# Register tables of a graph kernel's SAGE items laid out at a stride of eight words per turn

## The reference, cut to what matters

```
x: (6250, 128); src, dst: (100000,), sorted by dst; edge attributes: (100000, 16)
h = x                                            # three SAGE layers
for i in range(3):
    agg = segment_sum(h[src], dst); cnt = segment_sum(1, dst)
    h = (agg / clip(cnt, 1)) @ Wl[i] + bl[i] + h @ Wr[i]      # relu after the first two
x = layernorm(x + h)
z = concat(x[dst], x[src], edge_attr)            # one gated convolution
msg = sigmoid(z @ Wf.T + bf) * softplus(z @ Ws.T + bs)
agg = segment_sum(msg, dst)                      # batch norm, + x, layer norm, relu, + x
out = layernorm(x + that)
```

## Time and profile before

| what | value |
|---|---|
| median of 3 runs | 3572.85 us (3572.25 to 3573.68) |
| span of the profiled execution | 4974.4 us |
| time around that span | not recorded |
| first gather, first item of layer 0 | 63.9 us, 147.4 us |
| last gather of layer 2 | 3206.7 us |
| convolution's gathers | 3321.2 to 4818.0 us |

### The profile page before, as it was taken

How to read it: one execution, slowest core, us unless ns; L and a number is a source line. 1 busy time by engine, 2 the same in 40 slices (tenths; PEclk the granted TensorE clock), 3 DMA queues, 4 the chain that set the end, 5 groups by cost and what they waited for, 6 DMA issues and landing times. The chain is left out here.

```text
span 4974.4 us, 71543 instructions
## 1 busy us (share of the span) xinstructions
PE 3115.4 (63%) x16221; PEld 2251.0 (45%) x16222; DVE 2208.2 (44%) x5207; ACT 1206.7 (24%) x1906; POOL 2285.5 (46%) x2399
## 2 busy tenths in 40 slices
PE   4457677556366665463566664566777677777775
PEld 4334444445244443462344444544555455555553
DVE  5633333334411212354333333455666566556667
ACT  1112222101000000000000000035555555556665
POOL 2245445462355554533555555425455555444530
PEclk7678888767677777776787776687888788888887
DMA  3242323211333433113455542143333333222321
GB/s 95 77 132 90 100 87 101 73 41 46 89 103 105 108 106 90 40 38 115 147 157 149 149 139 74 36 126 89 86 87 85 87 85 87 80 81 82 89 61 41
DMA packets 345804, 454.70 MB, mean 91 GB/s; under 512 B 135431, under 2 KB 260386, under 8 KB 342099
## 3 DMA queue, kind: packets, MB, share of 16 engines
q0 software_dynamic: 88624, 207.58, 15.5%
q10 hardware_dynamic: 101984, 181.27, 11.4%
q1 hardware_dynamic: 155092, 64.77, 5.0%
HBM read 357.03 MB, written 101.90 MB: 92 GB/s over the span
## 5 line engine op out<-in xcount | busy, mean ns | idle before, releaser
L722 POOL DMA_INDIRECT shared<-y_dram,idx x1584 | 1514.9, 956 | 1604.7 <-DMA idx<-ea_sb 995.4
L909 PE MATMUL ps<-shared,work 128*128 x4368 | 786.2, 330 | 558.7 <-issue 463.2
L762 POOL DMA_INDIRECT shared<-q_dram,idx x784 | 753.6, 961 | 762.7 <-SPq L618 523.7
L909 PEld LDWEIGHTS ps<-shared,work 128*128 128x128 f32 x4368 | 709.3, 239 | 642.6 <-issue 631.4
L1961 DVE TENSOR_TENSOR acc<-acc,ps 128x129 f32 x546 | 156.0, 286 | 1577.4 <-remote 771.3
L1113 PE MATMUL ps<-pq,work 128*128 x1664 | 584.0, 453 | 146.6 <-issue 57.9
L928 PE MATMUL ps<-pq,work 128*128 128x385 bf16 x1456 | 335.8, 376 | 214.7 <-issue 119.3
L1113 PEld LDWEIGHTS ps<-pq,work 128*128 128x128 f32 x1664 | 299.8, 225 | 257.4 <-issue 201.2
L2250 DVE TENSOR_TENSOR work<-ps,shared 128x256 f32<-128x256 f32 x832 | 294.9, 417 | 248.6 <-PE ps L1116 94.8
L1264 ACT CAST work<-ps 128x300 bf16<-128x300 f32 (+1 forms) x520 | 175.1, 423 | 618.0 <-PE ps L900 322.8
L1123 PE MATMUL ps<-ident,work 128*128 128x128 f32 x832 | 152.9, 315 | 273.7 <-DVE work L2264 252.5
(11 more groups left out here) (356 smaller groups left out, 4062.7 us busy)
## 6 DMA issues: line engine op xcount, KB each, us to landing
work<-counts_dram ACTq DMA_DIRECT2D x156, 384.0 KB
counts_dram<-work ACTq DMA_DIRECT2D x26, 1568.0 KB
shared<-y_dram,idx POOLq DMA_INDIRECT x1584
ea_parts<-work ACTq DMA_DIRECT2D x128, 196.0 KB
ea_sb<-ea_parts SPq DMA_DIRECT2D x196, 128.0 KB
work<-counts_dram ACTq DMA_DIRECT2D x52, 416.0 KB
shared<-q_dram,idx POOLq DMA_INDIRECT x784
y_dram<-work SPq DMA_DIRECT2D x21, 448.0 KB, 3.1
```

The costliest lines, as they stand in the source:

```text
L722: pool.indirect_dma_start(msg[:, u, 0:F], None, y_dram, bass.IndirectOffsetOnAxis(ap=idx[:, u:u + 1], axis=0)).then_inc(s_quad[q], 16)
L762: pool.indirect_dma_start(q_ring[:, u * 2 * F:(u + 1) * 2 * F], None, q_dram, bass.IndirectOffsetOnAxis(ap=idx[:, u:u + 1], axis=0)).then_ ...
L909: last = te.matmul(ps[:, SUM_BANKS[i], 0:FA], lhsT=oh4[:, OH_SLOTS[i], u, :], rhs=shared[:, bass.ds(place + u * FA, FA)], start=u == 0, st ...
```

## The change

The tables in `q_regs` are no longer a copy of the twelve rows. Each table that is read by turns has eight words per turn, of which seven are used, and begins at a multiple of four words. Nine copies on SyncE's queue, each from a part of one row, fill it in the place of one. Every load of seven words becomes a load of four and a load of three, each from a multiple of four words; SyncE's load of twelve becomes three of four. VectorE's three or two first columns have places of their own. The semaphore `tab_back` counts eight copies more. The arithmetic on data, the order of the items and all other instructions are as before.

```diff
+WIDE = 8
...
+TURNS_ALL = TURNS + DTURNS
+CONV_TURNS = NQ // RC - 1
+NEEDED_AT = 0
+PLACES_AT = NEEDED_AT + TURNS * WIDE
+COLS_AT = PLACES_AT + TURNS_ALL * WIDE
+PAIR_COLS_AT = COLS_AT + TURNS * WIDE
+FIRST_COLS_AT = PAIR_COLS_AT + DTURNS * WIDE
+FIRST_PAIR_COLS_AT = FIRST_COLS_AT + 4
+SUMS_AT = FIRST_PAIR_COLS_AT + 4
+SUMMED_AT = SUMS_AT + TURNS_ALL * WIDE
+CONV_DONE_AT = SUMMED_AT + QG
+Q_WORDS = CONV_DONE_AT + CONV_TURNS * WIDE
+Q_TABLES = [(NEEDED_AT, 0, 0, TURNS, IT, WIDE), (PLACES_AT, 1, 0, TURNS_ALL, IT, WIDE), (COLS_AT, 2, OHS - 1, TURNS, IT, WIDE),
+            (PAIR_COLS_AT, 2, NI1 + LOOK, DTURNS, IT, WIDE), (FIRST_COLS_AT, 2, 0, 1, OHS - 1, OHS - 1), (FIRST_PAIR_COLS_AT, 2, NI1, 1, LOOK, LOOK),
+            (SUMS_AT, 3, 0, TURNS_ALL, IT, WIDE), (SUMMED_AT + RQ - AHEAD, 4, 0, 1, QG - RQ + AHEAD, QG), (CONV_DONE_AT, 5, 0, CONV_TURNS, RC, WIDE)]
+TAB_Q = 16 + 16 * len(Q_TABLES)
+TAB_ALL = TAB_Q + 32
...
-        q_regs = sb("q_regs", [1, 6 * NIC * P], i32)
+        q_regs = sb("q_regs", [1, Q_WORDS], i32)
...
-            sp.dma_start(q_regs[:, :], q_regs_dram.rearrange("r p -> (r p)").rearrange("(o k) -> o k", o=1))\
-                .then_inc(s["tab_back"], 16)
+            for at_, row_, first_, turns_, n_, wide_ in Q_TABLES:
+                from_dram = bass.AP(q_regs_dram.tensor, q_regs_dram.offset + row_ * NIC * P + first_, [[NIC * P, 1], [n_, turns_], [1, n_]])
+                sp.dma_start(q_regs[0:1, at_:at_ + turns_ * wide_].rearrange("o (t e) -> o t e", e=wide_)[:, :, 0:n_] if turns_ > 1
+                             else q_regs[0:1, at_:at_ + n_].rearrange("o (t e) -> o t e", e=n_), from_dram).then_inc(s["tab_back"], 16)
...
             def load_items(first, a, b):
-                sp.reg_load(l_regs[a:b], q_regs[0:1, bass.ds(first, b - a)])
+                for k in range(a - a % 4, b, 4):
+                    lo, hi = max(a, k), min(b, k + 4)
+                    sp.reg_load(l_regs[lo:hi], q_regs[0:1, bass.ds(first + lo, hi - lo)])
...
                 def load_turn(it):
-                    pe.reg_load(t_regs, q_regs[0:1, bass.ds(it * IT, IT)])
-                    pe.reg_load(g_regs, q_regs[0:1, bass.ds(it * IT + NIC * P, IT)])
+                    for k in range(0, IT, 4):
+                        pe.reg_load(t_regs[k:k + 4], q_regs[0:1, bass.ds(it * WIDE + (NEEDED_AT + k), min(4, IT - k))])
+                        pe.reg_load(g_regs[k:k + 4], q_regs[0:1, bass.ds(it * WIDE + (PLACES_AT + k), min(4, IT - k))])
...
             def load_columns(first, n):
-                dve.reg_load(c_regs[0:n], q_regs[0:1, bass.ds(first, n)])
+                for k in range(0, n, 4):
+                    dve.reg_load(c_regs[k:min(k + 4, n)], q_regs[0:1, bass.ds(first + k, min(4, n - k))])
```

More of the change, by code:

```diff
@@ L544, in turn @@
                     n = RQ if not isinstance(it, int) or it == 0 else RQ - AHEAD
-                    first = it * RQ + (4 * NIC * P + AHEAD - RQ)
+                    first = it * RQ + SUMMED_AT
                     if isinstance(it, int) and it == 0:
-                        done = [None] * (RQ - AHEAD) + load_items(4 * NIC * P, RQ - AHEAD, RQ)
+                        done = [None] * (RQ - AHEAD) + load_items(SUMMED_AT, RQ - AHEAD, RQ)
                     else:
@@ L589, in _ @@
                 sp.sem_inc(s["q_free"], 1)
-            sp.wait_ge(s["tab_back"], 64)
-            sp.wait_ge(s["tab_back"], 32)
+            sp.wait_ge(s["tab_back"], TAB_ALL)
+            sp.wait_ge(s["tab_back"], TAB_Q)
             sp.wait_ge(s["x1_ready"], NCH)
@@ L630, in needed @@
             def needed(m):
-                sp.reg_load(n_regs, q_regs[0:1, bass.ds(m * RC + (5 * NIC * P - RC), RC)])
+                for k in range(0, RC, 4):
+                    sp.reg_load(n_regs[k:k + 4], q_regs[0:1, bass.ds(m * WIDE + (CONV_DONE_AT - WIDE + k), min(4, RC - k))])
                 for q in range(RC):
@@ L932, in load_pairs @@
                 def load_pairs(turn):
-                    pe.reg_load(d_regs, q_regs[0:1, bass.ds(turn * IT + (NIC * P + NI1), IT)])
+                    for k in range(0, IT, 4):
+                        pe.reg_load(d_regs[k:k + 4], q_regs[0:1, bass.ds(turn * WIDE + (PLACES_AT + TURNS * WIDE + k), min(4, IT - k))])
                     return [pe.snap(r, min_val=0, max_val=(NGR - PT) * FA) for r in d_regs]
@@ L1072, in _ @@
             pe.wait_ge(s["we_in"], 16 * len(EA_GROUPS))
-            pe.wait_ge(s["tab_back"], 64)
+            pe.wait_ge(s["tab_back"], TAB_ALL)
             pe.wait_ge(s["p_done"], NCH * 4 + 4)
@@ L1210, in _ @@
                 first_res_copy(it)
-            act.wait_ge(s["tab_back"], 32)
+            act.wait_ge(s["tab_back"], TAB_Q)
             act.wait_ge(s["loads"], LOADS * 16)
@@ L1952, in load_turn @@
             def load_turn(it):
-                dve.reg_load(a_regs, q_regs[0:1, bass.ds(it * IT + 3 * NIC * P, IT)])
+                for k in range(0, IT, 4):
+                    dve.reg_load(a_regs[k:k + 4], q_regs[0:1, bass.ds(it * WIDE + (SUMS_AT + k), min(4, IT - k))])
                 sums = [dve.snap(r, min_val=0, max_val=(NW - 1) * FA) for r in a_regs]
-                return sums, load_columns(it * IT + (2 * NIC * P + OHS - 1), IT)
+                return sums, load_columns(it * WIDE + COLS_AT, IT)
             def add_item(layer, it, i, sums, columns):
@@ L1979, in load_pairs @@
             def load_pairs(turn):
-                dve.reg_load(b_regs, q_regs[0:1, bass.ds(turn * IT + (3 * NIC * P + NI1), IT)])
-                dve.reg_load(f_regs, q_regs[0:1, bass.ds(turn * IT + (2 * NIC * P + NI1 + LOOK), IT)])
+                for k in range(0, IT, 4):
+                    dve.reg_load(b_regs[k:k + 4], q_regs[0:1, bass.ds(turn * WIDE + (SUMS_AT + TURNS * WIDE + k), min(4, IT - k))])
+                    dve.reg_load(f_regs[k:k + 4], q_regs[0:1, bass.ds(turn * WIDE + (PAIR_COLS_AT + k), min(4, IT - k))])
                 return ([dve.snap(r, min_val=0, max_val=(NW - 1) * FA) for r in b_regs],
@@ L2222, in _ @@
             dve.wait_ge(s["x_kept"], NCH + 1)
-            dve.wait_ge(s["tab_back"], 64)
+            dve.wait_ge(s["tab_back"], TAB_ALL)
             dve.wait_ge(s["dlo_ready"], 1)
```

12 lines of the change are left out of this document (6 added, 6 removed).

## The result

Before: 3572.55 us median (3570.32 to 3573.68, 4 runs). After: 3553.85 us (3552.20 to 3556.01, 4 runs). Ratio 0.9947, 95% interval 0.9933 to 0.9962: 18.7 us less, 0.52%. The forecast was 3562, with a range of 3530 to 3574.

A forecast was written before the change was run, and what follows sets the result against it. GpSimd was taken to bind layers 1 and 2, TensorE and VectorE layer 0's woven part. Terms 7 + 1 + 1 + 1 - 1 = 9 us, plus 2 for partly missing cover, gave -11: 3562 us, range 3530 to 3574.

The forecast's parts named there:

- Bound by GpSimd in layers 1 and 2: Layers 1 and 2: GpSimd's gathers need 600 us, TensorE and VectorE 557, so 43 us a layer hide shorter loads.
- the rival that the engines bind everywhere: All layers: TensorE and VectorE set the pace, GpSimd's gaps being the profile's; 41 us gained, 3532 us; chance 0.30.
- The price of a load: Loads by turns: four aligned words 0.342 us, three 0.774 on VectorE; 0.33 and 0.81 on TensorE.
- The rival by which the change does nothing: Table loads: words come singly or the start is not aligned; layer 0's woven turns lose 13 us, 3586; chance 0.02.
- The two run side by side at a boundary, and both get shorter alike, so 7 us a layer: Woven turns' boundaries: TensorE's and VectorE's loads overlap and shorten equally; 7 us, counted in full for layer 0.
- Layer 0's dense part, gain 1: Layer 0's nine dense turns: loads save 7 us, but GpSimd's 161 us cover most; 1 us gained.
- Layers 1 and 2, gain 1 each: Layers 1 and 2: only stretches before the first freed slot and behind the last gather gain; 1 us each.
- The start, cost 1 (0 to 1.5, far bound 10.6): Start on SyncE's queue: eight more table copies take 2.0 to 3.9 us, partly hidden; 1 us lost.
- My own sign of being wrong: Layer 0's start: a first item more than 2 us later would show the forecast wrong.
- Nothing reaches the end: Layer 0's woven part: something else holds it, ScalarE's evictions or the ring; time stays 3572 us; chance 0.08.
- slower by the nine copies: Start: nine copies in 161 pieces delay VectorE's first one-hots and layer 0 by 10.6 us; 3583 us; chance 0.10.
- The model of the whole time: Whole kernel: stage times summed as a check, 698 us for layer 0, 700 for each next, leaving 1111 for the convolution.

The follow-up runs named there:

- the kernel before kept busy: The kernel before with four added products ahead of each of TensorE's two loads in layer 0's woven turns: 3569.55 us, ratio 0.9983.
- repeats: The changed kernel with added one-word register loads that appear in no trace, in layer 0 or in layers 1 and 2: 3551.21 and 3554.43 us.
- the clean execution: The kernel before, unedited, profiled a second time without the stalls of the first profile: 3572.97 us, span 3571.2 us.

## Why the prediction came out as it did

The sign, the place and the size within the range were right; the sum was not. It said 11 us less, 9 of them from its terms, and 18.7 were measured.

- **Bound by GpSimd in layers 1 and 2**: right, and the rival that the engines bind everywhere (chance 0.30) is out. Changed, slower and faster loads all leave item 0 to the last gather within some 4 us of the kernel before, in both layers. The cover is larger than I had it: the gathers have only 12 us of lead on item 0 (923.0 and 935.1 before), not 48 gathers, so they need 655 us and not 600.
- **The price of a load**: right for VectorE (0.34 to 0.35 for four; three 0.74 to 0.755 for 0.774), for TensorE's four 0.335. TensorE's three, which I took at 0.81 between 0.73 and 1.37, are 0.772. The rival by which the change does nothing, and with it a price by the register alone, is out: 0.34 us for four.
- **"The two run side by side at a boundary, and both get shorter alike, so 7 us a layer"** is the step that failed, and this term, 7 us for layer 0's woven part, measured 24.0. I had looked at one boundary, that of the earlier trace rows, and it is one of two kinds: in the loop's middle TensorE is late, at its end VectorE. So the savings add up, but each counts only at its own kind of boundary. In the middle TensorE's loads give 5.8 us. At the end VectorE's loads give 3.2 over six passes (0.54 each), not 7.1, which is their saving at all boundaries. The largest part stood in no term: VectorE's branch back, taken six times in this layer and 1.34 us cheaper each time with the changed code, 8.0 us. These two prices make 11.2 where the six passes measured 10.8. Outside the loop, ahead of turn 2, 2.2 us more are gained that no run traces to a cause. Between the boundaries 5.4 us are left, for which the clock, whose low stretches behind TensorE's stands shrink (9.1 us less busy time), is the likely cause: by the kernel before kept busy it is worth 4.4, an estimate.
- **Layer 0's dense part, gain 1**: 2.4 longer (repeats 2.0 and -0.1). GpSimd covers it, as I wrote, but it takes 179.5 us, not 157 to 161.
- **Layers 1 and 2, gain 1 each**: 1.6 and 0.2. **The convolution, 0**: 0.7 longer, nothing.
- **SyncE, 0**: nothing is to be seen; its four words take 0.298 us.
- **The start, cost 1 (0 to 1.5, far bound 10.6)**: the copies take 0.65 us each to issue, above the 0.49 I had taken (the far bound of 1.6 holds), so the last is issued 5.2 us after the first, not 2 to 4, and VectorE starts 4.4 us later. My own sign of being wrong, item 0 more than 2 us late, came true. The gain of layer 0 was larger than this miss. With the nine copies alone the run was 1.4 us slower at 2.5 us on item 0, within its error of nothing as of 2.5; but its copies take 2.61 us where the changed kernel's take 5.88, so it doesn't bound the change's own start.
- **Nothing reaches the end** and **slower by the nine copies** are out by the ratio; the latter had the right mechanism at 4.4 us instead of 10.6.
- **The model of the whole time** closed on errors that cancel: item 0 at 147 (119 in the clean execution), woven 527 (594), dense 161 (179.5), convolution 1111 (1043). That a total closes says little about its terms. The forecast's nearness has some luck in it too: layer 0's woven part gave 17 us more than its term, and the start and the dense part took back 3.4 each.

What stays open: why VectorE's branch back is shorter with more instructions in the loop. No kernel moved the loop without changing the loads, so it is a correlation over thirteen profiles. A load of eight with the shorter branch was not tried; if it can be had, some 8 us more (6 x 1.4, an estimate) are in reach in layer 0. So the change's gain is not all the worth of its layout: about a third of layer 0's comes from a shorter branch that may not come along in another kernel.

## What to carry to other kernels

Ask of each boundary of an unrolled loop which engine is late there, its end apart from its middle: savings on two engines add up where each one is late at a boundary of its own. Load registers from multiples of four words and in whole fours, rounding seven up to eight, but only where the engine that loads is what others wait for: behind back-to-back gathers the same saving was worth nothing. Look at what a loop's branch back costs before and after an edit; it can move by more than the edit was to bring. A test that adds work must show that work in its trace: loads of registers that nobody reads were not there, products into columns that nobody reads were.

## What the runs showed of the hardware

- Register loads on VectorE and TensorE in us: one word 0.31, three 0.74 to 0.77, four 0.34, seven 1.03 to 1.06 from a multiple of four words and 1.62 to 1.70 otherwise, eight 0.59. Whole aligned fours cost about 0.25 on top of the first, single words 0.23 each.
- VectorE's branch back in a loop of 308 to 332 recorded instructions takes 6.1 to 7.9 us, in loops of 101 to 142 0.3. With 308 it was dearer than with 316 or 332 in all thirteen profiles, by some 1.4 us counted from the last instruction ahead of it.
- After TensorE stands for 2.7 to 3.5 us its products run at 1.2 GHz for 2 to 3 us; with products put into the stand the low stretches all but vanish from turn 1 on (51 low products for 215, 48 for 128, most of them in turn 0).
- Of nine copies on one queue, the six in pieces of 28 bytes took 0.66 to 0.90 us each to issue, the other three 0.24 to 0.43; together 5.88 us. With every table in one piece the nine took 0.25 each, 2.61.
